# Three graph-attention units in one pipeline on Trainium2: an additive unit woven between the rows of a head, heads' results kept transposed, and the first head projected one turn early

## The chip, the cores and the metric

The kernel runs on one core of a Trainium2 chip, in one launch. The time is the device time in microseconds (us). Three runs of the kernel before took 5892.9, 5901.94 and 5911.97 us, so the median is 5901.94 us. One more execution was profiled.

TensorE is called PE, VectorE DVE, ScalarE ACT, GpSimd POOL and SyncE SP (it issues the DMAs). DVE and ACT read PSUM; POOL works on SBUF.

## The reference

For 8 batches of 2048 nodes with 64 features, four layers follow each other, each with a residual and a layer norm. The first (a gated sum) is a kernel part of its own that is not changed. The other three are:

```python
x = _layernorm(x + _L1_gnn_ref(x, adj, ...))   # 4 heads and a second attention over them
x = _layernorm(x + _L2_gnn_ref(x, adj, ...))   # additive attention, slope 0.01
x = _layernorm(x + _L3_gnn_ref(x, adj, ...))   # additive attention, slope 0.2

def _gat_layer(h, mask, b):                    # L1
    scores = where(mask, h @ h.T, NEG)
    return softmax(scores) @ h + b
z   = leaky_relu(concat_of_4_heads, 0.2)       # each head: h = x @ Wh[u].T, bias bh[u]
h2  = z @ Wo.T                                 # then _gat_layer(h2, mask, bo) again

e   = leaky_relu(h @ a1 + (h @ a2).T)          # L2, L3: an N x N matrix from two vectors
out = softmax(where(mask, e, NEG)) @ h
```

## The kernel before, in words

An N x N attention is worked off in **row blocks** of 128 rows by 2048 columns, 16 of them per unit. There are seven units per batch: the heads 0 to 3, their second layer `GAT2`, and the additive units `ADD1` and `ADD2`. Main-loop turn b runs `GAT2`, `ADD1`, `ADD2` of batch b and the four heads of batch b+1, 112 row blocks in all; there are seven turns, with a prologue (the heads of batch 0) and an epilogue (the last three units of batch 7).

The order of the rows is a list written out by hand (`loop_order`), and so is the step of each side task (`main_loop`). Each engine has its own queue and goes through the same steps. In step s it does its share for row s and for rows that are a few steps behind:

- *scores*, step s: for a head or `GAT2` PE makes the scores in PSUM tile `pss` (`dot_products`, L1027 and L1028, four 512-column pairs in two halves). For an additive row there is no matmul: ACT writes both halves of `pss` one step earlier (`lift_row`, L1208), and POOL adds the mask to `sr` in `rows` (`mask_row`, L863; for `ADD2` also L860 and L867). DVE then reads each half, masks it and takes the maximum (L1314), and ACT takes the exponential of the whole row (L1228).
- *turn*, step s+2: PE transposes the row in four groups into the PSUM tiles `tp0` and `tp1` (L1039). ACT (L1181) and DVE (L1326) copy the groups to `pt`: two each for a head or `GAT2` row, one and three for an additive row. A tile must be copied before it is used again.
- *sum*, steps s+3 and s+4 of every second row: PE multiplies a pair of rows with the values `hn` into `po` (L1059). ACT copies it to `ot` (`take_sums`, L1189).
- *turn back*, step s+5: PE transposes `ot` into the shared PSUM tile `px` (L1047), and ACT copies that to `ob` (`take_back`, L1196), behind the exponential of its step.
- *finish*, step s+6: POOL scales by the reciprocals `rc` (DVE, L1340), adds the bias and writes `z` (heads) or `y`.

Side tasks go through `px` too, one at a time. `xn` transposes a quarter of the input of the heads (L951). `proj` makes h of a unit (L985), which ACT and DVE split in a high and a low part for exact scores (L1148, L1150, L1151; L1278, L1279), and SP mirrors across the partition halves (`mirror_halves`). `hn` transposes it (L995). `z0` and `z1` transpose `z` for the projection of `GAT2` (L969, copies L1140). `xt`, `h`, `r` prepare an additive unit. `la` to `ld`, `ra` and `rb` are the residuals and layer norms on DVE and POOL. A task's step is the number in front of its name; .5 puts it late in the step.

Eight rows of the next turn's `GAT2` belong to the end of a turn (`AHEAD`), so the loop's own branch lies between rows 7 and 8 of `GAT2`.

## Time and profile before

| | |
|---|---|
| median of three runs | 5901.94 us |
| the profiled execution | 5898.7 us |
| its span on the core, first to last instruction | 5896.9 us |
| mean granted TensorE clock | 0.965 of full speed |
| busy: PE, DVE, ACT, POOL | 91%, 72%, 64%, 32% |

Busy time is what an engine's own instructions cover; several engines work at once. A row block starts here where its exponential starts on ACT (L1228), 896 in all, so the stretch of a unit runs from its first exponential to the next unit's. Turn 1 of the loop (the second) goes from 1359.8 to 2052.7 us. Times of an instruction stand beside the idle time of its engine just before it and what ended that.

### The profile page before, as it was taken

To read this page: it belongs to the slowest core of one execution; us is meant where nothing else is said; L and a number is where in the kernel's file an instruction comes from. 1 tells how busy PE (TensorE), PEld (TensorE's weight loads), DVE (VectorE), ACT (ScalarE), POOL (GpSimd) and SP (SyncE) were. 2 spreads that over 40 slices of the span, in tenths; PEclk is the share of its full clock that TensorE was granted. 3 is DMA by queue.
4 is the path that set the end of the run, shared out by engine and by line. 5 is a ranking of instruction groups with operands and counts; after the bars stand their busy time and mean duration, and the time that the engine had idled before them with its cause. 6 is when DMAs were issued, how large, how long until landed. Compare 5 with 4: busy or idle time off the path is not lost.

```text
span 5896.9 us, 163797 instructions
## 1 busy us (share of the span) xinstructions
PE 5353.8 (91%) x52610; PEld 4553.0 (77%) x52610; DVE 4219.7 (72%) x7321; ACT 3775.6 (64%) x5553; POOL 1881.5 (32%) x1724
## 2 busy tenths in 40 slices
PE   8499899989999898998989899998989989899966
PEld 7388787877788787887878777886878878787755
DVE  5666577667776778667786677767787677866766
ACT  3265567566766767666676667667576675766665
POOL 4300034042510525024250434206150152503366
PEclk9699999999999999999999999999999999999988
DMA  5200000000000000000000010000000001000000
GB/s 176 58 13 9 16 13 9 9 9 20 9 9 9 11 22 5 13 9 15 18 5 13 6 24 9 9 9 10 19 9 13 6 12 24 5 13 5 13 1 5
DMA packets 124202, 97.07 MB, mean 16 GB/s; under 512 B 94432, under 2 KB 97248, under 8 KB 123360
## 3 DMA queue, kind: packets, MB, share of 16 engines
q1 hardware_dynamic: 123360, 86.24, 5.9%
q8 instruction: 480, 7.86, 0.6%
q14 instruction: 362, 2.97, 0.2%
HBM read 35.35 MB, written 8.91 MB: 8 GB/s over the span
## 4 chain that ended last, share of the span: by engine, by line
PE 72%; issue 8%; DVE 5%; ACT 4%; DVEq 4%; POOLq 2%; POOL 1%; ACTq 0%; DMA 0%; SPq 0%
PE po L1059 23%; PE tp L1039 23%; PE pss L1027 10%; PE pss L1028 10%; DVEq L255 3%; ACT rows L1228 2%; POOLq L255 2%; DVE rows L1314 2%; PE px L985 2%; PE px L1047 2%; DVE pt L1326 1%; PE px L1002 1%; ACT pss L1208 1%; PE px L959 1%; PE px L969 1%
## 5 line engine op out<-in xcount | busy, mean ns | idle before, releaser
L1039 PE MATMUL tp<-ident,rows 128*128 128x128 f32 x14336 | 1992.8, 279 | 244.5 <-DVE pt L1326 193.5
L1326 DVE COPY pt<-tp 128x512 f32<-128x512 f32 x2048 | 1339.6, 686 | 957.7 <-PE tp L1039 942.3
L1228 ACT ACTIVATE rows<-rows,nm 128x2048 f32<-128x2048 f32 x896 | 1794.6, 2003 | 327.8 <-DVE nm L1314 315.3
L1039 PEld LDWEIGHTS tp<-ident,rows 128*128 128x128 f32 x14336 | 1611.8, 143 | 508.6 <-issue 457.7
L1059 PE MATMUL po<-pt,hn 128*64 128x128 f32 x28672 | 1805.4, 280 | 57.5 <-ACT ot L1189 57.3
L1059 PEld LDWEIGHTS po<-pt,hn 128*64 128x64 f32 x28672 | 1591.3, 139 | 217.3 <-issue 217.1
L1181 ACT COPY pt<-tp 128x512 f32<-128x512 f32 x1536 | 841.8, 590 | 708.9 <-PE tp L1039 702.1
L863 POOL TENSOR_TENSOR rows<-sr,mask 128x2048 f32<-128x2048 f32 x256 | 1049.2, 4101 | 154.1 <-PE tp L1039 145.9
L1027 PE MATMUL pss<-ha 128*128 128x512 f32 x2560 | 1064.5, 416 | 27.5 <-issue 13.9
L1028 PE MATMUL pss<-ha,hb 128*128 128x512 f32 x2560 | 1012.0, 395 | 0.0
L1314 DVE CUSTOM_DVE_ANT_0 rows<-pss,mask,nm 128x1024 f32<-128x1024 f32 x640 | 821.5, 1284 | 203.1 <-issue 201.2
L1314 DVE CUSTOM_DVE_ANT_0 rows<-pss,mask 128x1024 f32<-128x1024 f32 x640 | 782.4, 1223 | 84.2 <-PE pss L1028 36.9
L881 POOL TENSOR_TENSOR z<-ob,rc 128x128 f32<-128x128 f32 x256 | 102.8, 402 | 2197.8 <-ACT ob L1196 2185.1
L1208 ACT ACTIVATE pss<-sr,ls 128x1024 f32<-128x1024 f32 x512 | 567.5, 1123 | 97.1 <-DVE nm L1314 96.1
L1027 PEld LDWEIGHTS pss<-ha 128*128 128x128 f32 x2560 | 483.8, 189 | 116.5 <-issue 33.0
L1028 PEld LDWEIGHTS pss<-ha,hb 128*128 128x128 f32 x2560 | 485.1, 189 | 86.6
L1314 DVE CUSTOM_DVE_ANT_0 rows<-pss,rows,nm 128x1024 f32<-128x1024 f32 x256 | 328.6, 1284 | 78.7 <-issue 78.7
L832 POOL TENSOR_TENSOR st<-st,half_power 128x4 f32<-128x4 f32 x128 | 140.1, 1095 | 639.3 <-DVE st L280 639.3
L1314 DVE CUSTOM_DVE_ANT_0 rows<-pss,rows 128x1024 f32<-128x1024 f32 x256 | 309.9, 1211 | 45.9 <-POOL rows L867 26.6
L879 POOL TENSOR_TENSOR y<-ob,rc 128x128 f32<-128x128 f32 x128 | 51.6, 403 | 381.6 <-ACT ob L1196 364.8
L1148 ACT COPY hc<-px 128x512 f32<-128x512 f32 x80 | 46.9, 587 | 194.5 <-PE px L985 194.1
L1228 ACT ACTIVATION_READ_ACCUMULATOR rows<-rows,nm 128x1 f32 x896 | 167.9, 187 | 0.0
(108 smaller groups left out, 3220.2 us busy)
## 6 DMA issues: line engine op xcount, KB each, us to landing
hb<-ha SPq DMA_DIRECT2D x160, 128.0 KB, 2.3
ha<-hb SPq DMA_DIRECT2D x160, 128.0 KB, 2.3
adjb<-in_adj SPq DMA_DIRECT2D x32, 512.0 KB, 5.4
xin<-x SPq DMA_DIRECT2D x34, 128.0 KB, 2.3
xb<-in_x SPq DMA_DIRECT2D x16, 256.0 KB, 2.9
x<-t SPq DMA_DIRECT2D x16, 256.0 KB, 2.4
xb<-x SPq DMA_DIRECT2D x8, 512.0 KB, 3.9
out<-xb SPq DMA_DIRECT2D x32, 128.0 KB, 3.3
```

The lines of the kernel that those rows point to most:

```text
L255: eng.drain()
L832: nc.gpsimd.tensor_tensor(rstd, st[:, 1, blocks], half_power[:, 0:CH], ALU.pow)
L863: masked = nc.gpsimd.tensor_tensor(rows[:, row.slot, :], sr[:], mask[:, row.t, :], ALU.add)
L1027: nc.tensor.matmul(pss[:, cols], ha[i][:, rows_t], moving, start=True, stop=False)
L1028: last = nc.tensor.matmul(pss[:, cols], hb[i][:, rows_t], moving, start=False, stop=True)
L1039: last = nc.tensor.transpose(tp[q % 2][:, r * P:(r + 1) * P], rows[:, row.slot, jb * P:(jb + 1) * P], ident[:])
L1059: last = nc.tensor.matmul(po[side * D:(side + 1) * D, 0:P], hn[row.hn][:, r, :], pt[:, r, first + side, :], start=(r == 0), stop=(r == NB ...
L1181: nc.scalar.copy(pt[:, CH * q:CH * (q + 1), row.k % SLOTS, :], tp[q % 2][:].rearrange("p (j n) -> p j n", n=P)).then_inc(pt_act, 1)
L1208: nc.scalar.activation(pss[:, cols], sr[:, cols], ACT.Relu, scale=(1.0 - slope) / slope, bias=ls[:, row.unit - ADD1, row.t:row.t + 1]).the ...
L1228: nc.scalar.activation(rows[:, row.slot, :], rows[:, row.slot, :], ACT.Exp, scale=-1.0, bias=nm[:, row.place, 1:2], accum_out=rs[:, row.pl ...
L1314: nc.vector.tensor_tensor_reduce(out=scores, in0=pss[:, cols], in1=mask[:, row.t, cols] if row.gat else scores, scale=-1.0, scalar=(-2 * M ...
L1326: nc.vector.tensor_copy(pt[:, CH * q:CH * (q + 1), row.k % SLOTS, :], tp[q % 2][:].rearrange("p (j n) -> p j n", n=P)).then_inc(pt_dve, 1)
```

## The change

There are three parts.

1. *Order.* The rows of `ADD1` and of head 1 alternate in pairs. Two pairs of `ADD2` stand before and in the middle of head 3, and the other six behind it. The tasks get new steps: those of `ADD2` lie in head 2, the projection of `GAT2` at the end is spread, and DVE's part of `proj` is a task `low` of its own one step after `proj`.
2. *Heads' results stay transposed.* `po` holds a pair's sums already with the features on the partitions. Instead of turning them back and turning `z` again for `GAT2`'s projection, DVE now writes the reciprocals widened to 128 x 128 (`rcw`), PE turns these, and POOL multiplies `ot` with them and adds a bias per partition into `zt`. `z0` and `z1` go; `GAT2`'s projection multiplies with 64 partitions per head. `ot` is now read by POOL, so `take_sums` behind a head waits until POOL has finished. The reciprocals are taken two steps later.
3. *First head early.* `xn` and the projection of head 0 for the next turn are done in head 3 and not in `GAT2`; the prologue does them once more.

```diff
+    def behind_head(self, row):
+        earlier = [r for r in self.rows if r and r.k == row.k - 2]
+        return earlier[0].unit < H if earlier else False
+    def sequence(self):
+        return [(s, *task) for s in sorted(k for k in self.tasks if k != "before") for task in self.tasks[s]]
+def next_head(first):
+    tasks = [(first + (2, 3, 4, 5.5)[c], "xn", 0, c) for c in range(NC)]
+    for g in range(2):
+        at_g = first + 7 + 4 * g
+        tasks += [(at_g, "proj", 0, g), (at_g + 1, "low", 0, g), (at_g + 2, "hn", 0, g)]
+    return tasks
...
-    return pairs_of(GAT2, 2) + heads[0:8] + pairs_of(ADD1, 0) + heads[8:32] + pairs_of(ADD2, 0)
+    first, second = pairs_of(ADD1, 0), pairs_of(ADD2, 0)
+    turns_about = [pair for both in zip(first, heads[8:16]) for pair in both]
+    return pairs_of(GAT2, 2) + heads[0:8] + turns_about + heads[16:24] + second[0:1] + heads[24:28] + second[1:2] \
+        + heads[28:32] + second[2:8]
...
+    for unit, firsts in ((1, (21, 27)), (2, (46, 54)), (3, (74, 77))):
+        for g in range(2):
+            at_g = firsts[g]
+            tasks += [(at_g, "proj", unit, g), (at_g + 1, "low", unit, g), (at_g + 2, "hn", unit, g)]
-        tasks += [((8, 9, 10, 11.5)[c], "xn", 0, c)]
-        xt = (53, 59, 71, 81)[c]
+        xt = (65.5, 67.5, 69.5, 71.5)[c]
...
-    tasks += [(last - 4, "z0", GAT2, 0), (last - 3, "z1", GAT2, 0), (last, "z0", GAT2, 1), (last + 1, "z1", GAT2, 1)]
-    tasks += [(last + 2, "proj", GAT2, 0), (last + 4, "z0", GAT2, 2), (last + 5, "hn", GAT2, 0)]
-    tasks += [(last + 6, "z1", GAT2, 2), (last + 8, "z0", GAT2, 3), (last + 9, "z1", GAT2, 3)]
-    tasks += [(last + 10, "proj", GAT2, 1), (last + 11, "hn", GAT2, 1)]
+    tasks += next_head(80)
+    tasks += [(last + 1, "proj", GAT2, 0), (last + 2, "low", GAT2, 0), (last + 5, "hn", GAT2, 0)]
+    tasks += [(last + 9, "proj", GAT2, 1), (last + 10, "low", GAT2, 1), (last + 11, "hn", GAT2, 1)]
...
+        def own_columns(buf, half, unit, g, side):       # the mirrored columns; GAT2's lie in pieces of 128
+            both = buf[half, 2 * g * BANK:(2 * g + 2) * BANK]
+            if unit == GAT2:
+                return both.rearrange("p (q s n) -> p q s n", s=2, n=P)[:, :, side, :]
+            return both.rearrange("p (s q n) -> p s q n", s=2, n=P)[:, side]
...
+            def follow(segment, src):                     # SP: mirrors and loads in the steps' order
+                for _, name, unit, g in segment.sequence():
+                    if name == "low":
+                        mirror_halves(unit, g)
+                    elif name == "xn" and g < 2 and src is not None:
+                        load_chunk(src, g + 2)
...
+                if unit < H:
+                    dst = zt[:, unit, row.t // 2, :]
+                    nc.gpsimd.tensor_tensor(dst, ot[:], ob[:].rearrange("p r n -> p (r n)"), ALU.mult)
+                    drain_link(pool)
+                    nc.gpsimd.tensor_scalar(dst, dst, bhs[:, unit:unit + 1], None, ALU.add).then_inc(out_done, 1)
+                    return
...
-                wait(ot_c, ot_c.n + row.pair + 1)
+                if row.unit < H:
+                    wait(rc_c, rc_c.n + row.pair + 1)
+                    turned = rcw[:]
+                else:
+                    wait(ot_c, ot_c.n + row.pair + 1)
+                    turned = ot[:]
                 px_free()
-                nc.tensor.transpose(px[:, 0:P], ot[:], ident[:]).then_inc(back_ready, 1)
+                nc.tensor.transpose(px[:, 0:P], turned, ident[:]).then_inc(back_ready, 1)
...
-                    wait(back_c, back_c.n + row.pair)
+                    used = out_c if where[0].behind_head(row) else back_c
+                    wait(used, used.n + row.pair)
...
-                nc.vector.reciprocal(rc[:, pair], rs[:, pair]).then_inc(rc_ready, 1)
+                if row.unit >= H:
+                    nc.vector.reciprocal(rc[:, pair], rs[:, pair]).then_inc(rc_ready, 1)
+                    return
+                if row.pair or back_c.n:
+                    wait(back_c, back_c.n + row.pair)
+                nc.vector.reciprocal(rcw[:].rearrange("p (r n) -> p r n", r=2),
+                                     rs[:, pair].unsqueeze(2).to_broadcast([P, 2, D])).then_inc(rc_ready, 1)
```

Three places show how the instructions move. Before, on PE in step 9 of a turn (row 9 of `GAT2`; `xin` is the heads' input, `wts` their weights):

```order
L1028 MATMUL pss<-ha,hb 128x512
L951 MATMUL px<-ident,xin 64x128 x4
L260 REGISTER_ALU x2
L1039 MATMUL tp<-ident,rows 128x128 x4
L260 REGISTER_ALU
L1039 MATMUL tp<-ident,rows 128x128 x4
L1059 MATMUL po<-pt,hn 64x128 x16
L260 REGISTER_ALU
L985 MATMUL px<-xz,wts 64x128 x8
```

The same step after:

```order
L1064 MATMUL pss<-ha,hb 128x512
L279 REGISTER_ALU x2
L1075 MATMUL tp<-ident,rows 128x128 x4
L279 REGISTER_ALU
L1075 MATMUL tp<-ident,rows 128x128 x4
L1100 MATMUL po<-pt,hn 64x128 x16
```

The transpose of the input and the projection of head 0 are gone from `GAT2`.

On ACT inside `ADD1`, before (L1208 lifts a half, L1228 is the exponential, L1196 takes `ob`, L1181 copies a transposed group); the same rows come for all 16 row blocks:

```order
L1208 ACTIVATE pss<-sr,ls 128x1024
L260 REGISTER_ALU
L1208 ACTIVATE pss<-sr,ls 128x1024
L1228 ACTIVATE rows,rs<-rows,nm 128x2048
L1196 COPY ob<-px 128x128
L260 REGISTER_ALU
L1181 COPY pt<-tp 128x4x128
```

After, where a pair of head 1 follows a pair of `ADD1` (L1248, L1268, L1236, L1220 and L1229 are the lift, the exponential, and the copies to `ob`, `pt` and `ot`):

```order
L1248 ACTIVATE pss<-sr,ls 128x1024
L1268 ACTIVATE rows,rs<-rows,nm 128x2048
L1236 COPY ob<-px 128x128
L279 REGISTER_ALU
L1220 COPY pt<-tp 128x4x128
L279 REGISTER_ALU
L1220 COPY pt<-tp 128x4x128
L279 REGISTER_ALU
L1268 ACTIVATE rows,rs<-rows,nm 128x2048
```

Lifts now stand before two exponentials in four, and the copies of the head's rows come behind the exponential of the additive row.

On PE in `ADD2`, before, with the projection of `GAT2` (L985, weights `wo`) in the step after a turn back:

```order
L1047 MATMUL px<-ident,ot 128x128
L260 REGISTER_ALU
L1039 MATMUL tp<-ident,rows 128x128 x4
L260 REGISTER_ALU
L1039 MATMUL tp<-ident,rows 128x128 x4
L985 MATMUL px<-xz,wo 64x128 x16
L260 REGISTER_ALU x2
L1039 MATMUL tp<-ident,rows 128x128 x4
```

After, where a whole step without use of `px` (its sums are the L1100 row) lies ahead of it:

```order
L1100 MATMUL po<-pt,hn 64x128 x16
L279 REGISTER_ALU
L1075 MATMUL tp<-ident,rows 128x128 x4
L279 REGISTER_ALU
L1075 MATMUL tp<-ident,rows 128x128 x4
L279 REGISTER_ALU
L1021 MATMUL px<-zt,wo 64x128 x32
```

The projection has twice the matmuls and stands one step further from the last turn back.

## Rows read from the trace of the kernel before

**Rows 1.** The page: its span, and the chain of waits by engine.

```profile
span 5896.9 us, 163797 instructions
...
PE 72%; issue 8%; DVE 5%; ACT 4%; DVEq 4%; POOLq 2%; POOL 1%; ACTq 0%; DMA 0%; SPq 0%
```

**Rows 2.** Turn 1 by unit: GAT2, head 0, ADD1, heads 1 to 3, ADD2.

```profile
core 0: us, PE busy (x) PEld busy (x) DVE busy (x) ACT busy (x) POOL busy (x), PEclk, DMA share, GB/s
1359.80:1462.80 103.00, 98.19 (x964) 83.85 (x962) 76.11 (x139) 60.79 (x96) 18.23 (x29) 1.00 0.11 25
1462.80:1566.70 103.90, 102.46 (x1020) 87.62 (x1015) 75.08 (x138) 67.33 (x110) 28.54 (x34) 1.00 0.05 12
1566.70:1651.90 85.20, 70.37 (x781) 56.53 (x780) 74.88 (x133) 73.89 (x95) 65.19 (x29) 1.00 0.01 2
1651.90:1750.00 98.10, 97.94 (x970) 84.64 (x970) 70.78 (x124) 60.24 (x97) 9.20 (x17) 1.00 0.05 13
1750.00:1846.50 96.50, 96.50 (x966) 83.55 (x962) 65.81 (x112) 59.24 (x93) 6.91 (x16) 1.00 0.05 13
1846.50:1942.50 96.00, 95.34 (x949) 82.78 (x945) 63.29 (x109) 60.31 (x93) 16.05 (x21) 1.00 0.01 2
1942.50:2052.70 110.20, 84.61 (x857) 71.74 (x859) 83.30 (x137) 81.15 (x106) 76.97 (x59) 0.88 0.06 14
```

**Rows 3.** Same view: 12 head rows, 4 of ADD1, 15 of ADD2 (epilogue).

```profile
539.34:607.80 68.46, 68.46 (x682) 59.57 (x680) 47.20 (x81) 39.85 (x61) 5.18 (x12) 1.00 0.01 2
1587.32:1608.12 20.80, 17.38 (x197) 13.91 (x195) 18.10 (x31) 19.35 (x25) 17.61 (x7) 1.00 0.01 2
5783.32:5869.69 86.37, 61.35 (x593) 49.50 (x595) 69.83 (x118) 69.71 (x84) 74.35 (x53) 0.86 0.02 4
```

**Rows 4.** Waits of PE in ADD2, turn 1: total, times, longest.

```profile
PE px L985 <- ACT ob L1196: 5.1, 2, 2.7
PE px L969 <- ACT ob L1196: 5.0, 3, 2.5
```

**Rows 5.** Timeline of ADD2, turn 1: start, duration, instruction.

```profile
1998.93 2.58 PE L985 MATMUL px<-xz,wo 128*64 128x128 f32 x32 [2.32 <-ACT ob L1196]
2011.97 4.06 POOL L863 TENSOR_TENSOR rows<-sr,mask 128x2048 f32<-128x2048 f32 x1
2012.12 4.19 DVE L269 SCALAR_TENSOR_TENSOR xb<-st,xb 128x256 f32<-128x256 f32 x1
```

**Rows 6.** Timeline of PE in GAT2 (loop branch, xn, projection) and head 3.

```profile
1403.72 0.47 PE L1027 MATMUL pss<-ha 128*128 128x512 f32 x1 [2.39 <-issue]
1411.86 0.60 PE L951 MATMUL px<-ident,xin 128*64 128x128 f32 x4
1415.16 1.09 PE L985 MATMUL px<-xz,wts 64*64 64x128 f32 x16
1930.75 0.48 PE L1027 MATMUL pss<-ha 128*128 128x512 f32 x1
1932.69 0.60 PE L969 MATMUL px<-ident,z 128*128 128x128 f32 x4
```

**Rows 7.** Groups of the page: busy time, mean ns, idle before.

```profile
L1326 DVE COPY pt<-tp 128x512 f32<-128x512 f32 x2048 | 1339.6, 686 | 957.7 <-PE tp L1039 942.3
L1228 ACT ACTIVATE rows<-rows,nm 128x2048 f32<-128x2048 f32 x896 | 1794.6, 2003 | 327.8 <-DVE nm L1314 315.3
L1181 ACT COPY pt<-tp 128x512 f32<-128x512 f32 x1536 | 841.8, 590 | 708.9 <-PE tp L1039 702.1
L1314 DVE CUSTOM_DVE_ANT_0 rows<-pss,mask,nm 128x1024 f32<-128x1024 f32 x640 | 821.5, 1284 | 203.1 <-issue 201.2
L1208 ACT ACTIVATE pss<-sr,ls 128x1024 f32<-128x1024 f32 x512 | 567.5, 1123 | 97.1 <-DVE nm L1314 96.1
```

**Rows 8.** Single lines, whole trace: shortest, median, longest ns.

```profile
L1340 DVE RECIPROCAL rc<-rs x448: 152/155/168, 281.3 to 5882.6; 128x2 f32<-128x2 f32 x150
L269 DVE SCALAR_TENSOR_TENSOR xb<-st,xb x96: 424/425/4251, 747.0 to 5891.0; 128x256 f32<-128x256 f32 x96
```

More of the change, by code:

```diff
@@ L984, in run_task @@
                                     weights, moving = wh[:, unit, :], xt[:, first:first + P]
-                                last = nc.tensor.matmul(px[side * D:(side + 1) * D, own], weights, moving,
-                                                        start=(k == 0), stop=(k == 1 or unit != GAT2))
+                                last = nc.tensor.matmul(px[part, own], weights, moving,
+                                                        start=(u == 0), stop=(u == heads - 1))
                     last.then_inc(proj_psum, 1)
@@ L1154, in run_task @@
                     both = hn[hn_of(unit)][:, 2 * CH * c:2 * CH * (c + 1), :]
-                    nc.scalar.copy(both.rearrange("p (s k) d -> p k s d", s=2),
+                    both = both.rearrange("p (k s) d -> p k s d" if unit == GAT2 else "p (s k) d -> p k s d", s=2)
+                    nc.scalar.copy(both,
                                    px[:].rearrange("p (k s d) -> p k s d", s=2, d=D)).then_inc(hn_ready, 1)
@@ L1329, in bend_block @@
             def bend_block(row):
-                part = z[:, row.t + 1 - CH:row.t + 1, row.unit * D:(row.unit + 1) * D]
+                part = zt[:, row.unit, (row.t + 1 - CH) // 2:(row.t + 1) // 2, :]
                 wait(out_c, out_c.n + row.pair + 1)
```

147 lines of the change are left out of this document (69 added, 78 removed).

## Prediction

> **What bounds the kernel now.** I read the page first [rows 1]: PE is in 72% of the chain of waits, the rest is scattered. A share over the whole span does not say where PE waits, so the second view is one turn of the loop by unit [rows 2]. The reader is to compare, in each row, PE's busy time with the length of the stretch. In heads 0 to 3 they are the same within 1.5 us (102.46 of 103.90, 97.94 of 98.10, 96.50 of 96.50, 95.34 of 96.00): PE bounds these, and nothing but less work on PE makes them shorter. In `GAT2` 4.8 us are open, in `ADD1` 14.8 and in `ADD2` 25.6. That is 47 us of 692.9, and almost all the change can get per turn.
>
> The third view gives the price of a row block without side tasks [rows 3]. A head row takes 68.46/12 = 5.71 us, with PE busy throughout. An `ADD1` row takes 20.80/4 = 5.20 us; there ACT is busy for 19.35 of 20.80 and PE for 17.38, so ACT sets the pace. An `ADD2` row, whose stretch holds residual tasks as well, takes 86.37/15 = 5.76 us; POOL, with a mask that has two small extra operations, is busy for 74.35. So a head row leaves ACT idle and an additive row leaves PE idle, and today they stand in separate blocks.
>
> The fourth view is what PE waits for in `ADD2` [rows 4]: five side tasks wait 10.1 us in all for `ob`. ACT copies `ob` only behind the exponential of the step, and the tasks stand one step behind a turn back. At full clock the projection takes 2.58 us behind such a wait of 2.32 us [rows 5].
>
> **The change, part by part, for one turn.** The sum goes stretch by stretch, against turn 1.
>
> *GAT2.* Four `xn` (0.60 each) and two projections (1.09) with their `hn` (as `xn`, 0.60) leave [rows 6]: 2.4 + 3.4 = 5.8 us of PE work, in a stretch where PE is nearly full, and with them some 1.2 us of waits for `px` and copies, my estimate. The 2.39 us behind the loop's branch [rows 6] stay. 103.0 becomes 96.0.
>
> *Head 0.* Its tasks are the same: 103.9 stays.
>
> *ADD1 and head 1 in pairs.* Take a group of two additive and two head rows. The dot products of a head row start at 1930.75 and end at 1932.69 [rows 6], 1.94 us, so an additive row costs PE 5.71 - 1.94 = 3.77, and the group 2 x 5.71 + 2 x 3.77 = 19.0 us. ACT needs 2 x (19.35/4 + 39.85/12) = 16.3. DVE needs 2 x (18.10/4 + 47.20/12) = 16.9, and four gaps between its two halves of a row at 203.1/640 = 0.32 [rows 7]: 18.2. So no engine alone needs over 19.0. But the queues are in order. On ACT the copies of the last head row's groups come behind two lifts (2.25), an exponential (2.00) and the copy of `ob`, as its order shows. Counted from PE's start of the first additive row, ACT still works 1.4 on the last head's exponential, then 1.2 on copies [rows 7], 2.3 on lifts, 2.2 on the exponential with its sum, 0.25 on `ob`, 0.6 on the copy PE waits for: 8.0. PE then needs 1.1 more, so it is through two additive rows at 9.1 and not at 7.5. With 0.4 for DVE's copies that is 2.0 of waiting: 21.0 a group. Today it costs 2 x 5.20 + 2 x 5.71 = 21.8. Eight groups take 168.0; unit 2's projection and `hn` add 3.4 and three residual tasks, by my estimate 1.0 each: 174.4. The bounds are 19.0 below and, if one DVE operation per group is held by POOL, 21.0 + 3.8 = 24.8 above; I take 21.0.
>
> *Head 2* now has four `xt`, `h`, `r` and two projections, the list of head 0: 103.9.
>
> *Head 3 with two pairs of ADD2.* 16 x 5.71 = 91.4, two pairs at 21.0 - 11.4 = 9.6 each, and the tasks moved here, which PE has no gap for: 5.8. Together 116.4.
>
> *The last 12 rows of ADD2.* 12 x 5.76 = 69.1. ACT's copies for two projections and two `hn` cost about 0.6 each, eight of them: 4.8. Both projections now come behind a step that leaves `px` alone (the order excerpts), so of the 10.1 us for `ob` I keep 2. Together 76.
>
> *GAT2's projection and z0, z1.* Eight transposes of 0.60 [rows 6] and eight copies on ACT go. The projection has 64 matmul records for 32: bounded below by the heads' rate, 16 records in 1.09, hence 4.4 us, and above by twice today's time, 5.2; so +1.8 to +2.6 twice. That cancels the transposes within 1.2 us, and both lie where PE has time. I count nothing.
>
> *Transposed results.* PE's turn back is the same instruction. On POOL the two operations keep 128 columns; masks and finish fit today's 74.35 of 86.37 [rows 3], and the cover is gone only in the tail, where four heads' pairs are finished behind a mask and `take_sums` waits for them. That wait is queued ahead of ACT's next copies; I leave it inside the 2 us above. The wide reciprocal is not in this trace. From below it is the 0.155 us of today's [rows 8], from above the 1.28 us of a DVE pass over 1024 columns [rows 7]. At DVE's rate in copies, 686 ns for 512 columns, 128 columns more are 0.17 us: I take 0.3. In head rows DVE is busy 3.9 of 5.71 us and hides all of the range; in a group, 18.2 becomes 18.4 to 19.3, which starts to bound only at the end.
>
> The page VectorE: DVE Perf Modes of the Trainium skill (First, the fixed hardware budget) says that a reciprocal is an iterative divide with a repeat count of 8. Were this paid per element, 128 columns would take eight passes, by that page's 0.96 GHz about 1.07 us, an estimate. The trace doesn't decide it: its reciprocals have two elements.
>
> *Low part of `proj` one step later, SP's new order.* DVE no longer waits at `proj` for ACT's high part; in head units PE hides that wait anyway. SP issues mirrors in the steps' order, and each has three steps (over 15 us) before its unit begins. Nothing.
>
> Sum: 96.0 + 103.9 + 174.4 + 103.9 + 116.4 + 76.0 = 670.6, against 692.9: 22.3 less, seven times: 156. The prologue does the first head once more (+5.8) and has no `z0`, `z1` (about -2). The epilogue keeps its order. So 5898.7 - 156 + 4 = 5747 us for an execution like the profiled one. The profiled one is 3 us under the median of 5901.94, and I predict 5748.
>
> **The rivals.** *The engines' own work bounds the mixture.* If the queues' slack (a head row takes ACT only 3.3 of 5.7 us) swallows the waits, a group costs 19.0, ten groups save 20 us more per turn and the time is 5748 - 140 = 5608; with half of it 5678. For it: PE is full in all heads in spite of in-order queues. Against: in `ADD1` ACT is not full either (19.35 of 20.80) although nothing else binds it.
>
> *The mixture gives nothing.* DVE is close to PE, residual tasks and low parts fall between masks, and the reciprocal may be long. At 22.8 a group, 1.8 x 10 x 7 = 126 is lost: 5874; at half of that 5811. The gains of `GAT2` and the tail stay.
>
> *A lock between POOL and DVE, slower than before.* In rows 5 DVE's L269, which takes two SBUF operands, starts 0.15 us behind a mask of POOL and lasts 4.19 us, though its median is 0.425 [rows 8]; it ends 0.3 behind the mask. Masks are now spread over twice as many rows. If the wide reciprocal is held in this way, once in each of ten groups, 3.8 x 10 = 38 us are added per turn against 22.3 gained: 5748 + 266 = 6014. It decides from 2.2 us a group on. Against it: 448 reciprocals took at most 168 ns [rows 8], those of the additive units with their masks included, so this instruction doesn't seem to share what is locked. The rule is in SBUF - State Buffer (SBUF: two separate sides) of the Trainium skill: a DVE operation with two SBUF inputs, or in a two-port mode, and a GpSimd one exclude each other for a whole instruction. The 4.19 us agree with the first half; whether a wide reciprocal is such a mode no run here shows.
>
> **How the numbers follow.** Within 0.3% (18 us) a measurement of this kernel can't tell a change. Forecast, 5700 to 5800: 0.58. Faster mixture: 0.15. Mixture without gain, still faster: 0.14. No change, because waits eat all: 0.04. Lock or another wait, slower: 0.09. So faster 0.87, same 0.04, slower 0.09. The range for 8 in 10 leaves out the lock, no change, and the far ends of the two middle cases: 5650 to 5840.
>
> **What would show it.** In the changed profile: a turn of 671 us; 96 us for `GAT2` with no L994 in it; groups of 21 us in the mixture, with PE waiting for ACT's L1220 in the second additive row; PE's waits for `ob` in the tail at 2 us; wide reciprocals at 0.3 us each. I am wrong if a group takes 22 or more, if DVE operations of 4 us appear in the mixture, or if head 2 grows beyond 104.

## The result, and the profile after

The changed kernel takes 5831.23 us (median of four runs, 5827.03 to 5836.67), the kernel before 5898.52 us over its four. The ratio is 0.988, with an interval from 0.986 to 0.990: faster, clear of noise, but by 67 us (1.2%) and not by the 154 of the prediction. The time lies outside the forecast of 5700 to 5800 and inside the wider range of 5650 to 5840. The profiled execution took 5827.03 us, against a sum of 5747.

The stretches of turn 1, cut at the exponentials as in [rows 2]: `GAT2`, head 0, `ADD1` with head 1, head 2, head 3 with two pairs of `ADD2` (20 rows), the last 12 rows.

```profile
span 5825.1 us, 163883 instructions
...
PE 76%; issue 6%; DVE 6%; DVEq 4%; ACT 2%; POOLq 2%; POOL 0%; SPq 0%; DMA 0%; ACTq 0%
```

```profile
core 0: us, PE busy (x) PEld busy (x) DVE busy (x) ACT busy (x) POOL busy (x), PEclk, DMA share, GB/s
1349.04:1446.34 97.30, 93.86 (x896) 80.24 (x896) 73.53 (x135) 53.79 (x83) 18.22 (x29) 0.98 0.06 14
1446.34:1554.84 108.50, 103.05 (x1021) 87.92 (x1017) 79.78 (x139) 67.79 (x110) 29.77 (x34) 1.00 0.05 12
1554.84:1734.20 179.36, 166.16 (x1720) 141.04 (x1720) 148.22 (x250) 130.64 (x182) 75.64 (x45) 0.98 0.03 8
1734.20:1838.24 104.04, 102.47 (x1013) 88.48 (x1012) 73.33 (x119) 68.40 (x113) 18.65 (x22) 1.00 0.05 12
1838.24:1961.70 123.46, 118.82 (x1223) 102.78 (x1222) 91.13 (x150) 80.87 (x121) 32.27 (x36) 0.99 0.05 13
1961.70:2031.84 70.14, 57.84 (x651) 47.74 (x652) 60.29 (x99) 57.49 (x76) 55.17 (x40) 0.98 0.08 21
```

| stretch | forecast | measured | miss |
|---|---|---|---|
| GAT2 | 96.0 | 97.3 | +1.3 |
| head 0 | 103.9 | 108.5 | +4.6 |
| ADD1 with head 1 | 174.4 | 179.4 | +5.0 |
| head 2 | 103.9 | 104.0 | +0.1 |
| head 3, two pairs of ADD2 | 116.4 | 123.5 | +7.1 |
| last 12 rows | 76.0 | 70.1 | -5.9 |
| the turn | 670.6 | 682.8 | +12.2 |

Over all seven turns 80 us separate the profiled execution from the sum, 11.4 a turn. The prologue grew by 3.6 us (first exponential of the loop at 677.8, before at 674.2), as forecast.

The page's groups that answer to [rows 7], and the single lines that answer to [rows 8]:

```profile
L1075 PE MATMUL tp<-ident,rows 128*128 128x128 f32 x14336 | 1970.0, 277 | 267.6 <-DVE pt L1368 217.7
L1268 ACT ACTIVATE rows<-rows,nm 128x2048 f32<-128x2048 f32 x896 | 1794.2, 2002 | 451.4 <-DVE nm L1356 444.9
L1368 DVE COPY pt<-tp 128x512 f32<-128x512 f32 x2048 | 1338.2, 687 | 848.5 <-PE tp L1075 834.5
```

```profile
L1387 DVE RECIPROCAL rcw<-rs x256: 940/943/956, 294.2 to 5393.6; 128x128 f32<-128x128 f32 x128
L288 DVE SCALAR_TENSOR_TENSOR xb<-st,xb x96: 424/425/427, 744.5 to 5819.2; 128x256 f32<-128x256 f32 x96
```

The durations of the old instructions did not change. The wide reciprocal takes 0.94 us and not 0.3, with almost no spread; and no `xb` operation of this line is held any more (its longest was 4251 ns before). Two other DVE operations are held in the last 12 rows, for 0.8 and 1.9 us a turn; none is in the mixture. PE's idle time before the transposes ends mostly with DVE's copies (217.7 us of 267.6), as it did before (193.5 of 244.5), so this share tells nothing of the mixture yet.

**The three places of the miss.** Head 0 first. In PE's timeline the task `r` of `ADD1` and the projection of head 1 both come at step 21, and both go through the one tile `px`. The same happens at step 29, with `hn` of the second projection (L1031):

```profile
1475.54 0.60 PE L1048 MATMUL px<-ident,rt 128*128 128x128 f32 x4
1477.24 1.09 PE L1021 MATMUL px<-xz,wts 64*64 64x128 f32 x16 [1.11 <-ACT sr L1206]
...
1531.48 0.60 PE L1048 MATMUL px<-ident,rt 128*128 128x128 f32 x4
1533.09 0.63 PE L1031 MATMUL px<-ident,hc 128*128 128x128 f32 x4 [1.02 <-ACT sr L1206]
```

PE waits 1.1 and 1.0 us for ACT to read `px`, but the interval between exponentials, 6.48 us for the row of step 20 before, is 10.07: ACT and DVE are late as well. In head 3 the second projection of the next turn's head 0 comes at step 91, one step behind a turn back:

```profile
1895.40 0.33 PE L1088 MATMUL px<-ident,rcw 128*128 128x128 f32 x1
1895.57 1.04 PE L1075 MATMUL tp<-ident,rows 128*128 128x128 f32 x8
1899.52 1.09 PE L1021 MATMUL px<-xz,wts 64*64 64x128 f32 x16 [2.91 <-ACT ob L1236]
```

The wait is the one of [rows 5], moved to another unit. Behind it the clock is at half for a while too (0.98 over rows 80 to 95). The first of the two early projections, at step 87, also stands behind a turn back, and PE does not wait there (it starts at 1874.37, 0.86 us after `ob` was taken): its rows are a head's, with no lift ahead of the exponential on ACT, while two lifts stand ahead of the one at step 91.

In the same stretch lies a piece of work that the prediction counted in the tail, the first projection of `GAT2`. It runs before the exponential of row 100 (at 1961.70):

```profile
1952.68 3.71 PE L1021 MATMUL px<-zt,wo 64*64 64x128 f32 x64
```

In the mixture the third view is the waits of PE, and what the groups cost. A group of four rows without a task, one with a residual task and a projection, and the same again but later in the turn:

```profile
PE tp L1075 <- DVE pt L1368: 12.9, 15, 1.9
PE tp L1075 <- ACT pt L1220: 0.3, 2, 0.2
```

```profile
1597.50:1618.60 21.10, 19.68 (x210) 16.61 (x208) 17.02 (x30) 16.20 (x24) 9.66 (x5) 1.00 0.01 2
1618.60:1644.50 25.90, 23.39 (x234) 19.97 (x234) 21.50 (x38) 18.55 (x27) 11.80 (x7) 0.93 0.09 22
...
1665.70:1690.00 24.30, 21.83 (x234) 18.51 (x234) 21.30 (x38) 18.54 (x27) 11.79 (x7) 1.00 0.10 24
```

The group of 21.1 us is the forecast one (21.0). PE is busy for 19.7 of it and waits 1.1 for DVE, and not, as I had worked out, 2.0 for ACT. The two loaded groups do the same work and differ by 1.6 us, and by the granted clock. PE's timeline at their start shows where; first the one that ends at 25.9:

```profile
1619.73 1.23 PE L1075 MATMUL tp<-ident,rows 128*128 128x128 f32 x8 [1.92 <-DVE pt L1368]
1620.89 3.26 PE L1100 MATMUL po<-pt,hn 128*64 128x128 f32 x32
...
1666.80 1.23 PE L1075 MATMUL tp<-ident,rows 128*128 128x128 f32 x8 [1.92 <-DVE pt L1368]
1667.95 1.97 PE L1100 MATMUL po<-pt,hn 128*64 128x128 f32 x32
```

Behind the same wait of 1.92 us the 32 matmuls of a pair's sum take 1.97 us once and 3.26 the other time; there the granted clock was 0.59 and 0.55 over the next 4 us, so mostly at half (1.2 of 2.4 GHz):

```profile
1621.00:1623.00 2.00, 2.00 (x24) 2.00 (x26) 1.61 (x4) 0.78 (x2) 1.05 (x2) 0.59 0.00 0
1623.00:1625.00 2.00, 2.00 (x17) 1.67 (x14) 1.02 (x3) 1.95 (x2) 0.62 (x1) 0.55 0.00 0
1625.00:1627.00 2.00, 2.00 (x13) 1.65 (x11) 1.75 (x4) 0.29 (x3) 1.03 (x2) 1.00 0.00 0
```

### The profile page after: what moved, and what is told of

It reads as the page before. It is cut to its first block, busy times and chain, and to the rows that moved or that the text cites. A ratio compares the mean times of both kernels' runs of the same rounds, so it can differ in the third digit from the quotient of the medians.

```text
span 5825.1 us, 163883 instructions
## 1 busy us (share of the span) xinstructions
PE 5324.7 (91%) x52922; PEld 4537.3 (78%) x52922; DVE 4374.1 (75%) x7325; ACT 3748.3 (64%) x5501; POOL 1946.7 (33%) x1724
## 4 chain that ended last, share of the span: by engine, by line
PE 76%; issue 6%; DVE 6%; DVEq 4%; ACT 2%; POOLq 2%; POOL 0%; SPq 0%; DMA 0%; ACTq 0%
PE po L1100 25%; PE tp L1075 24%; PE pss L1063 10%; PE pss L1064 10%; DVEq L274 3%; PE px L1021 2%; DVE pt L1368 2%; POOLq L274 2%; PE px L1088 2%; ACT rows L1268 1%; DVE rows L1356 1%; PE px L1038 1%; DVE rcw L1387 1%; PE px L1002 1%; PE px L1048 0%
## 5 line engine op out<-in xcount | busy, mean ns | idle before, releaser
L1075 PE MATMUL tp<-ident,rows 128*128 128x128 f32 x14336 | 1970.0, 277 | 267.6 <-DVE pt L1368 217.7
L1268 ACT ACTIVATE rows<-rows,nm 128x2048 f32<-128x2048 f32 x896 | 1794.2, 2002 | 451.4 <-DVE nm L1356 444.9
L1100 PE MATMUL po<-pt,hn 128*64 128x128 f32 x28672 | 1805.2, 280 | 31.7 <-ACT ot L1229 28.3
L1100 PEld LDWEIGHTS po<-pt,hn 128*64 128x64 f32 x28672 | 1590.2, 139 | 187.7 <-issue 187.5
L1220 ACT COPY pt<-tp 128x512 f32<-128x512 f32 x1536 | 840.3, 589 | 728.4 <-PE tp L1075 721.9
L913 POOL TENSOR_TENSOR zt<-ot,ob 128x128 f32<-128x128 f32 x256 | 123.6, 483 | 1683.6 <-ACT ob L1236 1683.6
L1248 ACT ACTIVATE pss<-sr,ls 128x1024 f32<-128x1024 f32 x512 | 569.6, 1121 | 111.4 <-DVE nm L1356 106.4
L1387 DVE RECIPROCAL rcw<-rs 128x128 f32<-128x128 f32 x256 | 241.7, 944 | 1.4 <-PE px L1088 0.5
L915 POOL TENSOR_SCALAR zt<-zt,bhs 128x128 f32<-128x128 f32 x256 | 154.8, 605 | 43.5 <-issue 43.5
```

The lines of the kernel that those rows point to most:

```text
L1075: last = nc.tensor.transpose(tp[q % 2][:, r * P:(r + 1) * P], rows[:, row.slot, jb * P:(jb + 1) * P], ident[:])
L1100: last = nc.tensor.matmul(po[side * D:(side + 1) * D, 0:P], hn[row.hn][:, r, :], pt[:, r, first + side, :], start=(r == 0), stop=(r == NB ...
L1220: nc.scalar.copy(pt[:, CH * q:CH * (q + 1), row.k % SLOTS, :], tp[q % 2][:].rearrange("p (j n) -> p j n", n=P)).then_inc(pt_act, 1)
L1248: nc.scalar.activation(pss[:, cols], sr[:, cols], ACT.Relu, scale=(1.0 - slope) / slope, bias=ls[:, row.unit - ADD1, row.t:row.t + 1]).the ...
L1268: nc.scalar.activation(rows[:, row.slot, :], rows[:, row.slot, :], ACT.Exp, scale=-1.0, bias=nm[:, row.place, 1:2], accum_out=rs[:, row.pl ...
L1387: nc.vector.reciprocal(rcw[:].rearrange("p (r n) -> p r n", r=2), rs[:, pair].unsqueeze(2).to_broadcast([P, 2, D])).then_inc(rc_ready, 1)
```

## The experiments

Unless said otherwise the base is the changed kernel, and the comparison is with its 5831 us. "Turn" is turn 1.

### The wide reciprocal and the lock

**m1: a narrow reciprocal and a copy.**

```diff
-                nc.vector.reciprocal(rcw[:]..., rs[:, pair].unsqueeze(2).to_broadcast([P, 2, D]))
+                nc.vector.reciprocal(rc[:, pair], rs[:, pair])
+                drain_link(dve)
+                nc.vector.tensor_copy(rcw[:]..., rc[:, pair].unsqueeze(2).to_broadcast([P, 2, D]))
```

> The changed kernel with the wide reciprocal (944 ns in its profile, 0.3 us in the prediction) replaced by a reciprocal of 128x2 and a DVE copy that widens it; all results are computed. Theory L (the length of the reciprocal took the missing gain): DVE is freed of about 0.6 us for each of 32 head pairs of a turn, 19 us per turn, and where PE waits for DVE's copies the turn gets 5 to 9 us shorter, 35 to 60 us in all (5770 to 5795). Theory T (the new places of the side tasks took it): DVE's idle time swallows most of it, at most 20 us in all (5811 or more). If the copy is held by POOL's masks (two-port mode), copies of over 1 us appear in the mixture and the time is above the changed kernel's.

Measured: 6038.4 us, ratio to the kernel before 1.022 (1.021 to 1.024), so 207 us slower than the change. The copy takes 0.23 us, except where a mask of POOL runs:

```profile
L1389 DVE COPY rcw<-rc x256: 226/228/3785, 293.5 to 5604.7; 128x128 f32<-128x128 f32 x128
```

```profile
1573.14 8.13 POOL L900 TENSOR_TENSOR rows<-sr,mask 128x2048 f32<-128x2048 f32 x2
...
1577.59 3.77 DVE L1389 COPY rcw<-rc 128x128 f32<-128x128 f32 x1
```

It ends at 1581.36, with the mask (1581.27). In turn 1 this happens nine times, eight of them in the mixture, by 2.2 to 3.5 us each, and the turn takes 713.5 us. The slower rival of the prediction exists, but for another instruction. In the changed kernel 56 of the 256 wide reciprocals lie wholly beside a mask, and the longest took 956 ns.

**m2: PE widens.** Two matmuls with one column of `rc`, broadcast, as weights and the identity as moving operand write the widened, turned reciprocals at once.

```diff
-                    turned = rcw[:]
+                    for side in range(2):
+                        one = rc[:, row.place - 1 + side:row.place + side]
+                        last = nc.tensor.matmul(px[side * D:(side + 1) * D, 0:P], one.to_broadcast([P, D]), ident[:], ...)
...
-                nc.vector.reciprocal(rcw[:]..., ...)
+                nc.vector.reciprocal(rc[:, pair], rs[:, pair]).then_inc(rc_ready, 1)
```

> The changed kernel with a reciprocal of 128x2 alone; PE widens it itself by two products with the identity, each reading one column broadcast to 64. DVE is freed of 0.8 us per head pair, PE gets up to 0.2 us more. Theory L: 35 to 60 us less than the changed kernel, by a few us more or less than the kernel in which a copy widens. Theory T: at most 20 us less; if PE's extra work in the heads, where it is full, counts in whole (256 pairs, up to 0.2 us), the time doesn't move or grows.

Measured: 5809.84 us, 0.984 (0.983 to 0.986): 21 us faster. A group without tasks stays at 21.06 us (its four rows 3.84, 4.95, 6.78, 5.49; the four such groups take 20.9 to 21.5), the mixture falls from 179.4 to 175.5. So 0.8 us of DVE work a group is free where no task stands beside it, and costs 3.8 us a turn where one does: the three loaded groups take 24.2, 23.9 and 21.2 us in place of 26.0, 24.4 and 23.0.

**m3: the reciprocal twice.** One more wide reciprocal into a scratch tile, ahead of the real one.

```diff
+                nc.vector.reciprocal(tmp[:, 0:2, :], rs[:, pair].unsqueeze(2).to_broadcast([P, 2, D]))
```

> The changed kernel with the wide reciprocal done twice (the first into scratch). DVE gets 0.94 us more per head pair, 30 us per turn. Theory L: the slope stays or grows, so at least 60 us more than the changed kernel, mostly in the mixture. Theory T: under 30 us more.

Measured: 6038.06 us, 1.023 (1.022 to 1.025): 207 us slower for 256 x 0.94 = 241 us of DVE work. A clean group becomes 21.9 us, the mixture 189.0, head 0 112.0 and the 20 rows of head 3 with `ADD2` 136.6, 13 more than with one. Part of it is not the reciprocal: other DVE operations with two SBUF inputs were pushed beside masks, and held by some 9 us in this turn (2.8 in the changed kernel), two of them (3.8 and 3.4) in those 20 rows. DVE has no room for a second one.

**m12: the kernel before with a scratch wide reciprocal.** The same line, for head rows, in the kernel before.

> The kernel before, with a wide reciprocal (128x128, 0.94 us) into scratch added for every head pair, beside its own. In the old order head rows leave DVE 1.7 of 5.7 us: if that hides it, the time grows by under 15 us (1.5 us per turn where head pairs are still finished in ADD1 and ADD2). If the queues' order makes DVE's length felt in head rows as well, 50 us or more.

Measured: 5946.46 us, 1.008 (1.006 to 1.009): 47 us slower. The four heads grow by 0.2 to 1.1 us each, 2.4 in all, for 30 us more of DVE work in the turn, so there it is nearly hidden, as forecast. But `ADD1`, which has hardly any of them, goes from 85.2 to 90.7 us:

```profile
1624.75 4.06 POOL L863 TENSOR_TENSOR rows<-sr,mask 128x2048 f32<-128x2048 f32 x1 [1.28 <-PE tp L1039]
1624.88 4.21 DVE L269 SCALAR_TENSOR_TENSOR xb<-st,xb 128x256 f32<-128x256 f32 x1
...
1629.84 0.45 PE L1039 MATMUL tp<-ident,rows 128*128 128x128 f32 x1 [5.27 <-DVE pt L1326]
```

A small shift put a residual operation 0.13 us behind a mask's start; it is held 3.8 us, and PE waits 5.27 us for DVE's copies.

### Where the tasks stand

**m4: head 1's projection off `r`.**

```diff
-    for unit, firsts in ((1, (21, 27)), (2, (46, 54)), (3, (74, 77))):
+    for g in range(2):
+        at_g = (22, 26)[g]
+        tasks += [(at_g, "proj", 1, g), (at_g + 1, "low", 1, g), (at_g + 1, "hn", 1, g)]
+    for unit, firsts in ((2, (46, 54)), (3, (74, 77))):
```

> The changed kernel with head 1's projection one step later (steps 22 and 26, low part and hn one step behind), so that it doesn't stand in the step of ADD1's r, where PE waited 1.1 us for px and DVE 2.5 and 3.2 us for PE. Theory T: head 0's stretch goes from 108.5 to about 104, 4 us per turn, 25 to 35 us in all (5795 to 5806). Theory L: the stretch is long because of eight reciprocals, so it stays above 107 and the time moves by under 10 us.

Measured: 5791.26 us, 0.981 (0.980 to 0.982): 40 us faster. Head 0 takes 103.8 us, some 31 of the 40 us over the seven turns. The edit takes both collisions away, the one at step 21 and the one of `hn` at step 29, and the two together are the whole miss of head 0. Rows 20 to 23 take 27.7 us for 30.4, rows 24 to 31 50.9 for 52.9. The wait at the first projection is gone from the timeline:

```profile
1478.05 0.39 PE L1067 MATMUL pss<-ha,hb 128*128 128x512 f32 x1
1478.36 1.09 PE L1024 MATMUL px<-xz,wts 64*64 64x128 f32 x16
```

**m9: m4, and the early projection of head 0 one step later.**

```diff
-        at_g = first + 7 + 4 * g
+        at_g = first + 7 + 5 * g
```

> The changed kernel with only two task moves: head 1's projection off r (as before), and head 0's second early projection one step later, behind a step without a turn back. ADD1's residual tasks and unit 2's projections stay where the changed kernel has them. Theory (the kernel with all tasks moved was slower only because two of its DVE operations were held by a mask, 3.9 us each, 7.8 us per turn): head 3's gain of 3 to 4 us per turn stays and the locks go, so 5765 to 5775. Rival: the gain in head 3 is given back in the tail, and the time stays at 5791.

Measured: 5768.46 us, 0.977 (0.976 to 0.979): 63 us faster than the change. The stretches of turn 1 (head 0, the mixture, head 3 with two pairs):

```profile
1438.50:1542.40 103.90, 102.47 (x1021) 87.76 (x1017) 79.67 (x139) 67.44 (x110) 29.45 (x34) 1.00 0.05 12
1542.40:1721.70 179.30, 166.13 (x1719) 141.01 (x1719) 148.30 (x250) 130.67 (x181) 75.70 (x45) 0.98 0.03 8
...
1825.80:1945.10 119.30, 117.18 (x1224) 101.31 (x1223) 91.15 (x150) 80.87 (x121) 32.38 (x36) 1.00 0.06 13
```

**m5: m9's moves, the residual tasks of `ADD1` two steps later, unit 2's projections at 50 and 58.**

```diff
-            end = at(order, unit, n + CH - 1)
+            end = at(order, unit, n + CH - 1) + (2 if unit == ADD1 and c < NC - 1 else 0)
...
-    for unit, firsts in ((2, (46, 54)), (3, (74, 77))):
+    for unit, firsts in ((2, (50, 58)), (3, (74, 77))):
```

> The kernel with the projection off r, and besides: ADD1's residual tasks ra and rb of the first three quarters two steps later, on the head rows of the mixture and not on the additive ones; unit 2's projections on steps 50 and 58; head 0's second early projection on step 92, a step that doesn't follow a turn back. Theory T (side tasks on additive rows cost their full DVE time, since DVE is never idle there: 2.9 us per group with a residual instead of the 1.0 predicted): the mixture goes from 179.4 to 173 to 175, head 3's stretch from 123.5 to about 120, so 50 to 65 us less than the changed kernel, 25 to 35 less than with the projection off r alone. Rival: DVE pays them anywhere in the mixture, and the time equals that of the projection off r within 10 us.

Measured: 5803.71 us, 0.984 (0.983 to 0.986), so 35 us slower than m9. In two of the three places one of the residual task's operations starts with a mask and is held:

```profile
1617.54 4.07 POOL L903 TENSOR_TENSOR rows<-sr,mask 128x2048 f32<-128x2048 f32 x1 [6.26 <-PE tp L1078]
1617.59 4.30 DVE L291 SCALAR_TENSOR_TENSOR xb<-st,xb 128x256 f32<-128x256 f32 x1
```

**m6: m5 with PE widening.** The edits of m5 and m2 together.

> The kernel with the tasks on head rows, and the narrow reciprocal widened by PE. If the two gains add (the narrow one was 21 us alone): about 5750. If the reciprocal only cost where residual tasks stood beside it on DVE: equal to the kernel with the tasks moved, within 8 us.

Measured: 5815.45 us, 0.986 (0.984 to 0.988): 12 us slower than m5, where the same edit gained 21 on the changed kernel. The same two operations are held (3.89 us each), and the mixture stays at 184.1 (184.7 in m5). What PE's matmuls cost is left: 1.3 us in rows 80 to 95 and 5 in the prologue.

**m13: short residual tasks.** m9, and in the loop DVE does the first three residual tasks of `ADD1` for one row block of four, so the output is incomplete.

```diff
+                if name in ("ra", "rb") and unit == ADD1 and c < NC - 1 and where[0] is LOOP:
+                    short = slice(c * CH, c * CH + 1)
...
```

> The kernel with both projections moved off their collisions, and of ADD1's first three residual tasks in the loop VectorE does one of four row blocks only (so the output is not the reference's). Theory: each of these tasks costs the mixture 2.9 us because VectorE is nearly full there, and not the 1.0 that the prediction took; without them the groups with a task fall from 24-26 to about 21.5 and the mixture from 179.4 to about 172 per turn: 5768 - 7 x 7 = about 5720 us. Rival: the long groups come from the masks of GpSimd and the queues' order at those rows, not from VectorE's work; then the mixture stays at 178 or more and the time at 5758 or more.

Measured: 5735.9 us, 0.974 (0.972 to 0.976): 33 us faster than m9, not 48. The mixture takes 174.9 us, not 172:

```profile
1540.70:1715.60 174.90, 162.86 (x1720) 138.12 (x1720) 144.95 (x250) 130.66 (x182) 75.64 (x45) 1.00 0.03 8
```

The loaded groups, 25.97 and 24.37 us in the changed kernel, are both 23.96 here, 2.9 above a clean one (21.1), and they keep their projection. So of the 24 to 26 us the residual task was the smaller part, and my theory of 2.9 us a task had put the projection's cost on it. The group with a residual task alone falls from 23.0 to 21.0; in m9 it is 21.5 in the five turns in which the clock stays up there, so the residual itself is 0.5 of this and the clock 1.5. And the clock is 1.00: PE's longest wait in front of a pair's sum is now 1.5 us.

```profile
1605.24 1.23 PE L1078 MATMUL tp<-ident,rows 128*128 128x128 f32 x8 [1.51 <-DVE pt L1383]
1606.40 1.97 PE L1103 MATMUL po<-pt,hn 128*64 128x128 f32 x32
```

**m14: the second half of a residual task one step later.** m9 with `rb` of these three tasks at +9.

```diff
+            ra, rb = (7, 9) if unit == ADD1 and c < NC - 1 else (7, 8)
```

> The kernel with both projections moved, and the second half (rb) of ADD1's first three residual tasks one step later, on a head's row, where VectorE has 1.8 us to spare. Theory: half of the 2.9 us a task is hidden: mixture 179.4 to about 175, 5768 - 30 = 5738 us. Rival: one of its operations with two SBUF inputs now starts beside a mask of GpSimd and is held 3.8 us, as happened when both halves were moved; then 5768 or more, with operations of 4 us in the mixture.

Measured: 5786.06 us, 0.982 (0.980 to 0.984): 18 us slower than m9, with a mixture of 181.5 us. It is the rival in small. The two head rows that take the task grow from 7.00 to 7.82 us, and the 0.82 is one operation of DVE's low part, also with two SBUF inputs, that now begins before a mask ends (at 1627.24) and takes 1.49 us for 0.68:

```profile
1623.14 4.10 POOL L904 TENSOR_TENSOR rows<-sr,mask 128x2048 f32<-128x2048 f32 x1
...
1626.30 1.49 DVE L1323 TENSOR_TENSOR hb<-hc,ha 64x512 fp32r<-64x512 f32 x1
```

The additive row ahead (6.41 us) does not shrink, so nothing was there to gain either.

### The parts of the change

**m7: the changed kernel with the old order of rows and tasks** (parts 2 and 3 stay).

```diff
-    return pairs_of(GAT2, 2) + heads[0:8] + turns_about + heads[16:24] + second[0:1] + heads[24:28] + second[1:2] ...
+    return pairs_of(GAT2, 2) + heads[0:8] + pairs_of(ADD1, 0) + heads[8:32] + pairs_of(ADD2, 0)
```

> The changed kernel with the old order of the units (ADD1 and ADD2 in one block each, ADD2's tasks as before); transposed results and the early head stay. From the prediction's terms a turn is 97 + 108.5 + 85 + 98 + 97 + 101 + 99, about 686, so 15 to 35 us more than the changed kernel: the new order itself is worth only that. If the mixture gives nothing, the time is equal within 10 us; if it gives all of the gain, it is 5890 or more.

Measured: 5902.43 us, 1.001 (1.000 to 1.002), 71 us over the change where I expected 15 to 35. The kernel as it stands gains nothing without the order, but this is no clean measure of the order. Its head 0 still has the collisions (108.1 us, 103.9 in the kernel before), and in `ADD1` a residual operation now falls beside a mask and takes 4.22 us for 0.42; that stretch is 93.1 us, where I expected 85. These two stretches lie 12 us a turn over the kernel before. What the order is worth by itself m15 tells.

**m8: all pairs of `ADD2` behind head 3.**

```diff
-    return ... + heads[16:24] + second[0:1] + heads[24:28] + second[1:2] + heads[28:32] + second[2:8]
+    return ... + heads[16:32] + second
```

> The changed kernel with all eight pairs of ADD2 behind head 3. By the prediction a pair in head 3 costs 9.6 us and one in the tail 11.5, so two pairs save 3.8 us per turn and this kernel is 20 to 35 us slower. By the profile of the changed kernel head 3's stretch is 7 us over its forecast: then this kernel is equal or up to 20 us faster.

Measured: 5844.29 us, 0.991 (0.989 to 0.993): the two pairs inside head 3 are worth 13 us, less than the prediction's terms (20 to 35) and not the loss that head 3's long stretch suggested.

**m11: part 3 undone.** `xn` and the projection of head 0 back in `GAT2` at their old steps, SP's loads with them, and no early head in the prologue.

```diff
-    tasks += next_head(80)
+    tasks += [((8, 9, 10, 11.5)[c], "xn", 0, c) for c in range(NC)]
+    tasks += [(9.5, "proj", 0, 0), (10, "low", 0, 0), (11, "hn", 0, 0), (12, "proj", 0, 1), ...]
```

> The changed kernel with part 3 undone: xn and head 0's projection in GAT2 as before the change; order and transposed results stay. From the prediction's terms GAT2 gets 6 to 7 us longer and head 3 5.8 shorter: within 10 us of the changed kernel. If moving head 0 is what the change lives on: 30 us or more slower.

Measured: 5802.62 us, 0.984 (0.982 to 0.985): 29 us faster than with part 3, where I expected a difference within 10. `GAT2` is 102.9 us, head 3 with the pairs falls by 8.7 (rows 80 to 95: 87.1 against 95.8).

**m16: m4 with part 3 undone.** The edits of m4 and m11.

> The changed kernel with head 1's projection off the r task (as in the 5791 us kernel) and the third part undone. If the two effects add (-40 and -29 us), 5762 us. Against the kernel with both projections moved (5768 us) this tells what the third part is worth when its projection does not collide: theory, nothing, because the 5.4 us a turn that GAT2 loses are 4.5 more in head 3, where TensorE is full too, and 5 us in the prologue; so 5760 to 5775. Rival: GAT2's rows have waits that hide part of the work, so the late head is better still, under 5755.

Measured: 5767.6 us, 0.979 (0.977 to 0.980), the same as m9 within the noise. So part 3, placed where its projection does not collide, is worth nothing: m9, which has it, takes 97.5 us in `GAT2` where m16 takes 103.4, but 91.6 against 87.0 in rows 80 to 95, and 6 more in the prologue (678.6 against 672.5 at the loop's first exponential).

**m15: the order alone.** Parts 2 and 3 undone: `z0`, `z1`, narrow reciprocals, the first head late.

> The first part alone: the changed order of rows and tasks, with the results of the heads turned back and z turned again as before, narrow reciprocals, and the first head's input and projection in GAT2 as before. Against the changed kernel without the third part (5803 us): theory, the transposed results are worth little, since the saved transposes lie where TensorE has time and the wide reciprocal costs 3 us a turn; then 5780 to 5805 us. Rival: the transposed results also took the waits for ob out of the tail (10 us a turn before), so without them the tail grows by 6 us or more a turn, and the time is 5830 us or more.

Measured: 5811.22 us, 0.986 (0.985 to 0.988), against 5802.62 for m11, which has part 2 besides. Part 2 is worth about 9 us (16 by the two ratios), in these profiles some 0.7 a turn (mean turn 678.8 against 678.1), hardly to be told from nothing. By stretch it is not nothing: without it the mixture is 3.4 us shorter (176.0) and the last 12 rows are 6.8 longer (76.0 against 69.2).

Against the kernel before (5894.89 us beside it) the first part alone is worth 84 us, more than the whole change. It is the order and its task steps that gain; the early head, as placed, gives 29 back.

**m10: m9 with PE widening**, the version that the experiments pointed to: the edits of m9 and m2.

> The same two moves, and the 128x2 reciprocal that PE widens. If the narrow reciprocal's 21 us add: 5745 to 5755. If its gain was that of a mixture whose tasks now lie otherwise: as the kernel with the two moves, within 8 us.

Measured: 5757.77 us, 0.976 (0.975 to 0.977), 11 us under m9, so half of the 21 adds. It is the fastest of all that compute everything: 73 us faster than the change and 142 faster than the kernel before. The mixture:

```profile
1535.90:1711.30 175.40, 162.97 (x1746) 138.46 (x1744) 142.23 (x250) 133.01 (x185) 78.47 (x46) 1.00 0.03 8
```

## Why the prediction was wrong

The change is faster, as forecast, and the way to the gain was right: PE's open time was there to be filled. But 67 us came of 154. The terms that failed are these: head 0 at 103.9 ("its tasks are the same"), which was 108.5 with two collisions in `px`; the tasks in the mixture, 6.4 us for two projections and three residuals, which cost 10.5 with the clock; and head 3 at 116.4, which left out a wait of 2.9 us at step 91 and counted `GAT2`'s first projection in another stretch. The tail was 5.9 us better than forecast and hid a part of that.

*GAT2, 96.0 against 97.3.* Right within 1.3 us. m11, with the work back in it, takes 102.9, as [rows 2] has it (103.0), so the size of what left is confirmed.

*"Head 0. Its tasks are the same: 103.9 stays."* This step failed, and m4 shows it: 4.6 us a turn, 31 of the 40 us that m4 gains. The tasks are the same, their steps are not. The diff moves head 1's projection from step 22 to 21, where `r` of `ADD1` stands (17 + 4), and `hn` of the second one from 27 to 29, where the last `r` stands (17 + 12); all of them need `px`. I had read which tasks a unit holds and not which of them now share a step.

*The mixture, 174.4 against 179.4.* The size of a clean group was right (21.0 against 21.1), and that is luck: PE's own work is 19.7 and not 19.0, its idle time 1.4 and not 2.0, and the engine behind it is another. Over the mixture PE waits for DVE, 12.9 us, and for ACT 0.3. It stays at 21.1 with 0.8 us of DVE work less (m2) and grows to 21.9 with 0.9 more (m3). So the term for ACT's queue in my sum is refuted, though its result came. What failed in the size are the tasks. A group with one projection and a shortened residual costs 2.86 us more than a clean one (m13), where I had 1.7 for projection and `hn`. A full residual beside it adds 0.4 us (24.37 against 23.96), which is less than the 1.0 I gave it. The rest is the clock. By groups: 8 x 21.1 = 168.8; 0.5 more in the first; 3.27 in each of two with a task and a projection (6.5); 1.6 for the clock in one of them; 1.9 in the last, where a residual is alone and the clock falls as well, behind a wait of 1.91 (a pair's sum takes 3.62 us for 1.97): 179.3. Without the long reciprocal (m2, m10, m15) or with less residual work (m13) the clock in the mixture of turn 1 is 0.99 or 1.00 and it takes 175 to 176 us, close to the forecast. The sign that I had named for being wrong, a group of 22 us or more, came in the three loaded groups alone.

*The wide reciprocal: "I take 0.3".* It takes 0.944 us, within the bounds of 0.155 to 1.28 but three times my value. I scaled from copies, by columns; this instruction does 128 columns in 0.94 us, 7.4 ns each, and 2 in 0.156. The Trainium skill, VectorE: DVE Perf Modes (First, the fixed hardware budget), has a repeat count of 8 for a reciprocal. The estimate from it was 1.07, and the measured 0.94, 12% under it, is far nearer to it than to my 0.3. The price is 21 us in all (m2) or 11 (m9 to m10), and it appears where the prediction said that the upper end "starts to bound": only beside tasks, and through PE's waits and the clock.

*Head 3, 116.4 against 123.5.* Of the 7.1 us, 4.2 are the second early projection behind a turn back and the clock behind it (m9, 119.3). Another 3.7 are the first projection of `GAT2`, which the sum had in the tail; it runs at full PE here. The rest was forecast well: m11, without the early tasks, takes 114.7, and 111.0 without that projection, against 16 rows and two pairs at 110.6; the early tasks add 4.5 (m9 against m11) where I had 5.8. The wait is that of [rows 4] and [rows 5], which I had used to forecast a gain in the tail and did not look for in the rows that the change adds to head 3.

*The tail, 76 against 70.1.* The waits of PE for `ob` are gone, not at 2 us but at zero:

```profile
PE tp L1075 <- DVE pt L1368: 9.5, 15, 1.9
PE po L1100 <- ACT ot L1229: 2.1, 3, 0.8
```

So 2 of the 5.9 us are here. One projection of the two was done before these rows began (3.7 us, above). And the price of 5.76 us a row was read in [rows 3] at a granted clock of 0.86; here it is 0.98. That the clock matters shows in m15, which turns `z` as before. Its last 12 rows against those of m11:

```profile
1948.02:2023.97 75.95, 61.31 (x635) 51.74 (x636) 58.18 (x99) 59.46 (x79) 55.92 (x42) 0.91 0.08 19
1951.87:2021.06 69.19, 56.46 (x650) 46.16 (x651) 60.27 (x99) 57.40 (x76) 55.12 (x40) 1.00 0.09 21
```

With fewer matmuls PE is busy 4.9 us longer in m15, at 0.91 for 1.00, and it waits 4.6 us for `ob` where m11 does not wait at all. So part 2 gains here, by the waits and by the clock that falls with them, and I had counted the waits alone. How the 5.9 us divide among the three no run separates.

*Part 3.* The terms (5.8 and some waits less in `GAT2`, 5.8 more in head 3) were nearly right (5.9 and 4.5), and that they all but cancel is in the prediction's own sum. The prologue takes the rest: m16 against m9 shows zero.

*The rivals.* "The mixture gives nothing", 5811 to 5874, holds the measured time, but for another reason than it gives: groups are at 21.1 and not at 22.8. That a DVE operation is held while a mask of POOL runs is shown (m1, m5, m12), and so is the size, up to 3.9 us for each; the instruction that I feared it for is not held. The Trainium skill, SBUF — State Buffer (SBUF: two separate sides), names two SBUF inputs or a two-port mode for this. The residual operations of m5 and m12 have two, and agree. The copy of m1 has one SBUF input and an SBUF output and is held too, 3785 ns against 228. Whether it runs in a two-port mode no run here shows.

*What stays open.* Why the clock falls behind one wait of 1.92 us and not behind the other: the groups ahead hold the same instructions, and from turn to turn of m9 it falls in the last group of the mixture twice and stays up five times. No run separates it. Nor is it shown why a projection with its `hn` costs 2.9 us in a group, for 1.7 of PE's work; its copies and DVE's low part (1.5 us) are the likely part.

## What to carry to other kernels

When tasks share a tile, list for each step of the new order which of them meet in it and which copy stands before them; two such collisions, in head 0 and in head 3, cost 63 us here, and moving the tasks by a step took them away. The same wait costs more where the copy stands behind additive rows' lifts than in a head. An operation that a nearly full engine hides in a clean stretch is paid in the stretch beside it that has a task, so the sum is to be made for the most loaded group and not for the mean one. And in a kernel with long GpSimd operations a shift of 0.1 us can hold a short VectorE one for 3.8 us: a change that touches neither (m12) can cost 5 us a turn by it.

## What was not expected of the hardware

- A VectorE reciprocal of 128 x 128 f32 takes 940 to 956 ns, of 128 x 2 156 ns. A copy of the same shape from SBUF takes 228 ns, if it is not held.
- While GpSimd works on a 128 x 2048 operation of 4.1 us, the copy is held up to 3785 ns, and the reciprocal, with the same broadcast input, never (56 lay wholly beside one).
- TensorE's clock fell from 2.4 to 1.2 GHz behind waits of PE of 1.9 us, and in m15 behind one of 1.76, so that 32 matmuls took 3.26 to 3.62 us in place of 1.97. Behind another wait of 1.92, and behind those of 1.5 in the mixture of m13, it did not.
